# Side jobs of an attention kernel moved to other places in its order of work

## The reference

```python
x = x + attn(layernorm(x))       # 16 heads of 8; k_rec, v_rec through a latent of 32; distance decay on the scores
x = x + ffn(layernorm(x))        # bf16 -> float8_e4m3 grid, times a 128x128 kernel, plus bias
scores = clip(q k^T * scale) * exp(-0.0001 * |i - j|);  out = softmax(scores) v;  out @ Wo
```

## Time and profile before

| | us |
|---|---|
| median of 3 runs | 591.28 |
| lowest and highest | 588.19, 592.32 |
| the profiled execution: its time | 588.45 |
| its span in the trace | 586.4 |

### The profile page before, as it was taken

The page is one execution under the profiler, slowest core; times in us unless marked ns, Lnnn a source line. Parts: engine busy times, 40 slices in busy tenths (PEclk is TensorE's granted clock), DMA queues, the critical chain, the costliest instruction groups (busy, mean ns, idle before and its releaser), DMA issues.

```text
span 586.4 us, 9462 instructions
## 1 busy us (share of the span) xinstructions
PE 502.4 (86%) x3515; PEld 117.1 (20%) x3515; DVE 321.0 (55%) x772; ACT 486.5 (83%) x523; POOL 179.4 (31%) x123
## 2 busy tenths in 40 slices
PE   2786988999999999999999999999999999999620
PEld 1321212222121221212121212221212111211110
DVE  5389343246645666545645766456644654455334
ACT  1465766799999998999999998999999999999600
POOL 2499400995100208790100228860100010001001
PEclk9998999999999999999999999999999999999955
DMA  6364890369899610667855202488667000100000
GB/s 197 108 216 153 247 185 1 113 175 239 296 245 195 137 45 4 219 225 210 225 125 116 65 6 87 156 308 205 131 132 165 7 6 7 41 5 5 25 4 21
DMA packets 46097, 74.07 MB, mean 126 GB/s; under 512 B 6176, under 2 KB 27360, under 8 KB 45920
## 3 DMA queue, kind: packets, MB, share of 16 engines
q1 hardware_dynamic: 44512, 72.70, 45.6%
q10 hardware_dynamic: 1536, 0.73, 0.5%
HBM read 35.40 MB, written 35.65 MB: 121 GB/s over the span
## 4 chain that ended last, share of the span: by engine, by line
PE 42%; ACT 28%; DVE 14%; issue 11%; DMA 2%; SPq 2%; POOL 0%; ACTq 0%; POOLq 0%; DVEq 0%
ACT probs L538 27%; PE ps L692 19%; PE ps L679 9%; PE ps L675 4%; DVE ps L880 3%; DVE pv_out L886 2%; DVE Qs L825 2%; PE ps L614 2%; PE ps L577 2%; PE ps L609 2%; PE ps L581 2%; PE ps L586 1%; DMA o_raw<-pv_out 1%; SPq L347 1%; DMA wv_s<-L_attn_Wv 1%
## 5 line engine op out<-in xcount | busy, mean ns | idle before, releaser
L538 ACT ACTIVATE probs<-ps 128x1024 f32<-128x1024 f32 x512 | 480.8, 1069 | 48.4 <-DVE ps L880 29.2
L692 PE MATMUL ps<-probs,V 128*9 128x512 f32 x2048 | 269.2, 597 | 9.7 <-DVE pv_out L886 3.9
L880 DVE TENSOR_TENSOR ps<-ps,consts 128x256 f32<-128x256 f32 (+1 forms) x256 | 142.6, 564 | 171.1 <-PE ps L679 150.3
L679 PE MATMUL ps<-Qs,Ks 64*128 64x512 bf16 x896 | 166.0, 385 | 18.9 <-ACT probs L538 9.0
L679 PEld LDWEIGHTS ps<-Qs,Ks 64*128 64x128 bf16 x896 | 40.3, 93 | 266.0 <-ACT probs L538 246.1
L465 POOL TENSOR_TENSOR xs<-xs,magic 128x512 f32<-128x512 f32 x8 | 10.2, 1277 | 247.6 <-DVE magic L938 247.6
L675 PE MATMUL ps<-Ks,Qs 32*128 32x512 f32 x256 | 38.3, 656 | 14.7 <-ACT probs L538 13.9
L692 PEld LDWEIGHTS ps<-probs,V 128*9 128x9 f32 x2048 | 31.3, 88 | 95.0 <-issue 53.5
L886 DVE COPY pv_out<-ps 105x512 f32<-105x512 f32 x32 | 22.0, 688 | 30.9 <-PE ps L692 30.9
L429 POOL TENSOR_TENSOR X<-X,mv 128x512 f32<-128x512 f32 x7 | 7.3, 1042 | 88.3 <-DVEq L1043 79.2
L440 POOL TENSOR_TENSOR parts<-sq,parts 128x768 bf16<-128x768 f32 (+1 forms) x16 | 31.5, 1968 | 1.3
(11 more groups left out here) (102 smaller groups left out, 271.0 us busy)
## 6 DMA issues: line engine op xcount, KB each, us to landing
Qs<-qp_dram SPq DMA_DIRECT2D x32, 512.0 KB, 8.9
qp_dram<-parts SPq DMA_DIRECT2D x16, 768.0 KB, 5.4
Ks<-kp_dram SPq DMA_DIRECT2D x32, 384.0 KB, 7.2
kp_dram<-parts SPq DMA_DIRECT2D x16, 576.0 KB, 4.2
qp_dram<-parts SPq DMA_DIRECT2D x8, 512.0 KB, 7.2
kp_dram<-parts SPq DMA_DIRECT2D x8, 384.0 KB, 4.8
X<-L_attn_x SPq DMA_DIRECT2D x4, 512.0 KB, 7.3
kt_dram<-kT SPq DMA_DIRECT2D x4, 512.0 KB, 9.4
```

The source lines that it names most:

```text
L538: nc.scalar.activation(probs[:, quad % RING, 2 * jp:2 * jp + 2, :].rearrange("p j n -> p (j n)"), ps_all[:, bank * CH:(bank + 2) * CH], AC ...
L679: last = nc.tensor.matmul(bank, Ks[half, g, jp, key_cols(v, kc)], Qs[half, g, jp, v, qh * CH:(qh + 1) * CH], start=True, stop=True)
L692: last = nc.tensor.matmul(pv[32 * j:32 * j + VW, :], V[:, unit // 2 * NB + kc, HG * j + g, :], probs[:, quad % RING, j, :], start=i == 0, ...
L880: nc.vector.tensor_tensor(own, own, factors, ALU.mult).then_inc(fixed, 1)
```

## The change

The table of jobs is written anew (`is_shared(unit)` is true for units 0 to 5), and the steps of VectorE that belong to it move with it. Quads of the unit in which the step is done, before and after:

| | before | after |
|---|---|---|
| sp, proj | 8, 10 | 10, 12 |
| xqT, y in units 1 to 5 | 26, 28 | 30, 2 of the next unit |
| xqT, y in units 6, 7 | 26, 28 | 28, 30 |
| T, T | 14, 16 | 14, 18 |
| k, k | 18, 20 | 22, 26 |
| q, q | 22, 24 | 28, 4 of the next unit |
| v, v | 30, 0 of the next unit | 6, 14 of the next unit |
| n | 18 of the second unit | 28 of the second unit |
| n of batch 0 | 26 | 20 |
| flags, flag | unit 5, 22, 24 | unit 6, 4, 6 |

```diff
 for _u in range(1, UNITS + 1):
-    JOBS += [(_u * UNIT_QUADS + _q, _k, _u - 1) for _q, _k in ((8, "sp"), (10, "proj"), (26, "xqT"), (28, "y"))]
+    JOBS += [(_u * UNIT_QUADS + _q, _k, _u - 1) for _q, _k in (
+        (10, "sp"), (12, "proj"), (30 if is_shared(_u) else 28, "xqT"), (34 if is_shared(_u) else 30, "y"))]
 for _b in range(B - 1):
     JOBS += [(_b * STREAM + _q, _k, 2 * (_b + 1) + _h) for _q, _k, _h in (
-        (14, "T", 0), (16, "T", 1), (18, "k", 0), (20, "k", 1), (22, "q", 0), (24, "q", 1), (30, "v", 0), (32, "v", 1))]
-    JOBS += [(_b * STREAM + 50, "n", _b + 1)]
-JOBS += [(2 * STREAM + 54, "flags", 0), (2 * STREAM + 56, "flag", 0)]
+        (14, "T", 0), (18, "T", 1), (22, "k", 0), (26, "k", 1), (28, "q", 0), (36, "q", 1), (38, "v", 0), (46, "v", 1))]
+    JOBS += [(_b * STREAM + 60, "n", _b + 1)]
+JOBS[2] = (20, "n", 0)
+JOBS += [(3 * STREAM + 4, "flags", 0), (3 * STREAM + 6, "flag", 0)]
...
             def prepare_rows(b, at):
-                if at < 2 or at > 11:
-                    return
-                if at == 2:
+                if at == 3:
                     dve.wait_ge(x_in[b], 16)
-                if at < 6:
-                    tile_stats(b, (2 * at - 4, 2 * at - 3))
-                elif at < 8:
-                    tile_moments(range(4 * at - 24, 4 * at - 20))
-                else:
-                    for i in range(3 * at - 24, 3 * at - 21):
-                        inverse_std_step(i, mv, rs)
+                    tile_stats(b, range(NB))
+                elif at == 5:
+                    tile_moments(range(NB))
+                for i in {5: range(5), 6: (5, 6), 8: (7, 8), 10: (9, 10), 11: (11,)}.get(at, ()):
+                    inverse_std_step(i, mv, rs)
...
-            def tail(unit, at):
-                if at == 6:
+            def tail(unit, at, late):
+                if at == 7:
                     invert_sums(unit)
-                elif at == 7:
                     widen_sums(unit)
-                elif at == 12:
+                elif at == 13:
                     row_stats(unit)
-                elif at == 13:
+                elif at == 15:
                     row_moments()
...
+                for i in {15: (0, 1, 2), 16: (3, 4), 18: (5, 6), 19: (7, 8), 20: (9, 10), 21: (11,)}.get(at, ()):
+                    inverse_std_step(i, mv2, rs2)
+                if at == 21:
+                    normalise_rows(unit, range(4))
+                elif at == 22:
                     divide_rows()
-                elif at == 21:
+                elif at == 23:
                     grid_of_rows(0)
                     grid_of_rows(1)
-                elif at == 24:
+                elif at == 27:
                     quantise(unit, 0)
+                if at == (28 if late else 27):
                     quantise(unit, 1)
-                elif at == 30:
+                if at == (35 if late else 31):
                     dve.wait_ge(y_ready, unit + 1)
                     add_bias()
                     result(unit)
...
                 if unit > 0:
-                    tail(unit - 1, at)
+                    tail(unit - 1, at, is_shared(unit))
+                if unit > 1:
+                    tail(unit - 2, at + UNIT_QUADS, is_shared(unit - 1))
```

More of the change, by code:

```diff
@@ L92, with is_shared @@
 JOBS = [(0, "v", 0), (2, "v", 1), (26, "n", 0)]
+def is_shared(unit):
+    return unit // 2 < B - 1
 for _u in range(1, UNITS + 1):
-    JOBS += [(_u * UNIT_QUADS + _q, _k, _u - 1) for _q, _k in ((8, "sp"), (10, "proj"), (26, "xqT"), (28, "y"))]
+    JOBS += [(_u * UNIT_QUADS + _q, _k, _u - 1) for _q, _k in (
+        (10, "sp"), (12, "proj"), (30 if is_shared(_u) else 28, "xqT"), (34 if is_shared(_u) else 30, "y"))]
 for _b in range(B - 1):
     JOBS += [(_b * STREAM + _q, _k, 2 * (_b + 1) + _h) for _q, _k, _h in (
-        (14, "T", 0), (16, "T", 1), (18, "k", 0), (20, "k", 1), (22, "q", 0), (24, "q", 1), (30, "v", 0), (32, "v", 1))]
-    JOBS += [(_b * STREAM + 50, "n", _b + 1)]
-JOBS += [(2 * STREAM + 54, "flags", 0), (2 * STREAM + 56, "flag", 0)]
+        (14, "T", 0), (18, "T", 1), (22, "k", 0), (26, "k", 1), (28, "q", 0), (36, "q", 1), (38, "v", 0), (46, "v", 1))]
+    JOBS += [(_b * STREAM + 60, "n", _b + 1)]
+JOBS[2] = (20, "n", 0)
+JOBS += [(3 * STREAM + 4, "flags", 0), (3 * STREAM + 6, "flag", 0)]
 JOBS.sort()
@@ L1028, in prepare_rows @@
             def prepare_rows(b, at):
-                if at < 2 or at > 11:
-                    return
-                if at == 2:
+                if at == 3:
                     dve.wait_ge(x_in[b], 16)
-                if at < 6:
-                    tile_stats(b, (2 * at - 4, 2 * at - 3))
-                elif at < 8:
-                    tile_moments(range(4 * at - 24, 4 * at - 20))
-                else:
-                    for i in range(3 * at - 24, 3 * at - 21):
-                        inverse_std_step(i, mv, rs)
-                    if at == 11:
-                        settle()
-                        dve.sem_inc(stats_ready, 1)
@@ L1045, in tail @@
-            def tail(unit, at):
-                if at == 6:
+                    tile_stats(b, range(NB))
[3 more added lines that the diff above has]
+                    inverse_std_step(i, mv, rs)
+                if at == 11:
+                    settle()
+                    dve.sem_inc(stats_ready, 1)
+            def tail(unit, at, late):
+                if at == 7:
@@ L1105, in finish @@
                 residual(unit)
-                for at in range(12, 22):
-                    tail(unit, at)
-                tail(unit, 24)
+                for at in range(13, 28):
+                    tail(unit, at, False)
                 empty_work("xqT", unit)
                 empty_work("y", unit)
-                tail(unit, 30)
+                tail(unit, 31, False)
             finish(last_unit)
```

## The result

The changed kernel takes 595.75 us, the median of 18 runs (592.29 to 598.79), beside 591.41 us for the kernel before on the same chips: ratio 1.0071, interval 1.0044 to 1.0098. That is 4.3 us slower where I had forecast 1 us faster. The time lies inside the stated range of 580 to 599, but the sum behind the forecast had the wrong sign. The ratios of the experiments leave out two executions, one of e6 and one of e7, that were over 1.5% above the fastest of their kernel. The profiled execution has a span of 590.7 us instead of 586.4.

What follows compares the result with a forecast made beforehand. ScalarE's exponentials were taken to pace units 1 to 7, TensorE unit 0. Terms -2.6 - 3.4 + 0 + 2.4 + 2.6 = -1.0 against the median 591.28 gave 590.3, stated as 590.0 us, range 580 to 599.

Steps and rivals of the forecast that it cites:

- The term of unit 0: Unit 0: VectorE steps ahead of quad 8's mask wait for GpSimd; 2.0 to 4.1 us later, taken 3.0.
- the terms as I listed them: Unit 0's jobs: v leaves 0.75, q 0.25; q, n pay 0.7 each, before 0.7 and nothing; k 0.35 less.
- rival B: Units 3 and 5: gather behind the stores lands 6.0 us after issue, `invert_sums` waits 3.9 more; +7.9, 598; chance 0.1.
- the predicted gather: Units 3 and 5: gather behind the stores starts at 7 to 8.3 us, delaying `invert_sums`; 0.5 to 2.7, taken 1.4.
- The 1.0 us for GpSimd: Units 1, 3, 5: later `queries` makes `widen_sums` and inverse steps meet GpSimd; 1.0 us each, bounds 0 and 3.
- my two terms for it: Unit 1: moved jobs 3.0 us by the same prices, meetings with GpSimd 1.0; booked 4.3 after, change 0.
- quad 3 of units 2 and 4: VectorE's y, eight statistics, bias and result take 3.5 us there, making quad 4's wide mask 1.4 us late.
- The pricing of a job: A job alone delays the masks behind it: some 0.35 us if the next are narrow, 0.5 if wide.
- Rival D: Units 1 to 7: starving is TensorE's total work, so 29.7 us stay and only waits come; about 600; chance 0.05.
- rival A: Units 0 to 5: new waits on GpSimd, gathers and quad 3 do not come; -12.6, 578.7, half 584; chance 0.27.
- Rival C: One VectorE step per GpSimd operation, not two: unit 0 4 us more, units 1, 3, 5 1 to 2; 596 to 599; 0.08.
- The signs that I had named for "right": Quads 9, 17, 25, 1 at 1.8 to 1.95; units 6, 7 near 59.1; late quad 8 mask; quad 3 idle; `rec` waiting.

Runs made afterwards that it cites:

- e6: Kernel of e1, in unit 0 moments and twelve steps in quads 12 and 13, T in 18 and 20, n in 12: 585.48 us, ratio 0.9943.
- e7: Kernel of e1, in a batch's second unit the load of group 2 issued behind the last gather: 585.76 us, ratio 0.9898.
- e3: Kernel before, with only the new quads of the row statistics: 594.60 us, ratio 1.0058.
- e1: Changed kernel with the row statistics (statistics, moments, twelve steps) back in their old quads: 589.80 us, ratio 0.9992.
- e4: Changed kernel with k in quads 20 and 22, q in 26 and 28 of a batch's first unit, n of batch 0 in 12: 590.33 us, ratio 0.9994.
- e2: Changed kernel with the gather issued ahead of the second half's stores of keys and queries in SP's queue: 592.88 us, ratio 1.0019.
- e9: Kernel of e8, with bias in quad 3 and result in quad 5 of the next unit, n of batch 0 in 14: 573.98 us, ratio 0.9748.
- e8: Kernel of e5 plus e6's late statistics, e7's load order, unit 0 jobs shifted, bias and result in quad 5 of the next unit: 584.42 us, ratio 0.9891.
- e5: Changed kernel with the edits of e1 and e4 together, nothing else: 586.27 us, ratio 0.9933.

## Why the prediction was wrong

Unit by unit, predicted and measured change in us (spans of the two profiled executions):

| | 0 | 1 | 2 | 3 | 4 | 5 | 6 | 7 | sum |
|---|---|---|---|---|---|---|---|---|---|
| predicted | +2.6 | 0 | -1.8 | +1.2 | -1.6 | +1.2 | -1.3 | -1.3 | -1.0 |
| measured | +5.6 | 0.0 | +1.8 | +0.4 | -2.2 | +0.4 | -1.0 | -0.9 | +4.1 |

**The term of unit 0 was too small: 4.8 us by e3, where I had taken 3.0.** The mechanism was right: seven steps ahead of the mask of quad 8, in pairs of which one is held by a GpSimd instruction. The mask came at 53.94 in e3, at the late end of my 52 to 54. In the changed kernel it came at 55.49, but 1.6 us of that is a fall of the clock at 30.9 us, which came by chance. Two things, here with the changed kernel's numbers, pushed it to the late end: one of the two `first_keys` of quad 6, which stand between the steps, waits for a GpSimd instruction of its own (2.87 us), and a GpSimd instruction also waits for it, so the chain that I followed was itself longer (L449 1.65 us instead of 1.04). The larger part of the miss lies behind the mask. I had quads 8 to 11 at 11.5 us, by the pitches of quads 16 to 19 at full clock; they took 12.6 in e3 and in the changed kernel. In e3 the steps there were through at 55.15, and VectorE then stood idle for 2.60 us until TensorE, at half clock from 49.7 to 59.9, had the next scores. In e6, with neither steps nor half clock there, the same quads took 11.5. So the clock, which falls to half in the long wait, is what I had left out; that it and not the steps makes these quads longer is read from the idle time and not shown by an edit. The changed kernel's unit 0 grew by 5.6 us: these 4.8, the 1.6 by chance, and less by the jobs moved out. For the jobs the terms as I listed them add up to -0.65 us where I booked -0.4; e1 has -0.5. The exclusive lock of the Trainium skill (SBUF — State Buffer, "Who interferes with whom") agrees with the rows: all 51 steps on eight elements that took over 0.4 us in the eleven traces ended 0.02 to 0.03 us behind a GpSimd instruction. The size of the loss had to come from the traces.

**The term of unit 2's gather was left out, and this turned the sign.** I let units 1, 3 and 5 bunch their loads "as they did in unit 1", in time, though the earlier trace rows had `rec` waiting 1.41 us in unit 2, booked nothing for it, and put the 6.0 us of the earlier trace rows aside as rival B, for units 3 and 5. It came in unit 2 instead, and as 10.1 us: the load of group 2 had its last DMA issued 5.6 us ahead of the gather before (176.06, 181.65) and 1.7 us ahead of it now (185.75, 187.49). e7 shows the order as the cause, e4 the late k and q; either removes the loss. Its price, 3.3 us in quad 7 and 0.8 in quad 10 behind the fall of the clock, is the 4.1 us by which unit 2 is longer than unit 4, and more than the distance of 3.6 between my -1.8 and the measured +1.8.

**Units 3 and 5** have the predicted gather (7 to 8.3 us into the unit, 7.4 measured) and landing (2.06, 2.07). It cost 2.2 us instead of 1.4, the issue taking 5.9 instead of 4.75 us. The 1.0 us for GpSimd did not add, since the widening falls into the same wait; e2, which takes the wait away, brings it back. In unit 1 it came (quads 7 and 15 lose 1.0 and 1.2 us), and the unit kept its length as forecast, though my two terms for it, 3.0 and 1.0, make 4.0 us and not the 4.3 that I booked.

**The gains were right within 0.6 us:** quad 3 of units 2 and 4 lost 1.2 us (1.4 predicted), units 6 and 7 come to 59.4 and 59.5 (59.1), unit 4 to 61.7 (62.3), copies cost nothing. The pricing of a job at 0.35 to 0.5 us by the masks behind it held: sp and proj cost unit 6 0.8 us (0.85). Rival D falls by units 6 and 7, rival A by unit 0. Rival B's slow landing did not come in units 3 and 5. Rival C's number, 596 to 599, is next to the measured 595.75, but by luck: two VectorE instructions went through for each of GpSimd's, as I had it, and not one. The signs that I had named for "right" came true, but none of them asked about unit 2's gather.

So the change does what it says to the collisions, and loses more elsewhere. e3 puts 3.4 us on the new places of the statistics; e1 shows that with the old ones the rest is worth nothing (0.9992). e4 and e7 show what late k and q and the load ahead of the gather take away. e9, 2.5% under the kernel before, has these two taken out, bias and result in two quads, and in unit 0 the statistics where GpSimd is quiet; what each of the four gives by itself within it is not measured.

## What to carry to other kernels

In an order written by hand, a step moved off a collision lands on something: ask for each moved VectorE instruction that works from SBUF to SBUF (here all but statistics, moments and reciprocals) what GpSimd does at that time, and keep at most one of them between two instructions that the bounding engine waits for. For each moved producer follow the issuing queue to the end: a small transfer behind a big load waits for the load (unit 2 here: `rec` went on 10.1 us behind the gather's issue in the changed kernel, and without a wait in e7). Tiny instructions are not cheap ahead of a critical one; put them where the other engine is quiet.

## What the runs showed of the hardware that I had not expected

VectorE instructions on 8 elements a partition, alone 0.17 us, took up to 2.3 us while GpSimd ran an instruction, and ended within 0.03 us of it; statistics, moments, reciprocals and everything that reads PSUM with at most one SBUF operand were untouched (the eight moments of quad 5 ran in 0.63 us beside L450, and a mask of 512 columns takes 0.70 us beside GpSimd as alone).

The granted clock fell to half (1.2 GHz) for 3.4, 6.8 or 10.2 us behind the long waits of TensorE, and the fall adds to the stall: quad 10 of the changed kernel's unit 2 took 0.8 us more than that of unit 4. One fall came by chance: between 28.7 and 30.9 us of the span, where all eleven profiled kernels have the same instructions in the same order, it came in five (changed, e2, e4, e7, e8), for 3.4 or 6.8 us, and cost quad 2 of unit 0 1.4 to 2.7 us more than in the other six. The scatter of some 6 us between runs of one kernel goes with the clock: e9's four runs at 573.4 to 574.2 us have a mean granted clock of 0.970 to 0.974, those at 578.2 and 579.9 one of 0.966 and 0.964. Of the 23 runs of the kernel before beside e5 the 14 up to 590.6 us have 0.968 to 0.972, the 9 from 591.3 us on 0.962 to 0.966. Where in these runs the clock fell is not known, since only one execution of each kernel has a trace.

What sets off the chance fall, and how much of each ratio above it carries, stays open.
